# First attention of a two-layer sequence kernel: queries turned once, row maxima put beside them by small transfers

## The reference, cut to what matters

```python
q = _apply_rope((x @ Wq).reshape(b, t, 32, 16).transpose(0, 2, 1, 3), cos, sin)
k = _apply_rope((x @ Wk).reshape(b, t, 8, 16).transpose(0, 2, 1, 3), cos, sin)
scores = jnp.einsum('bhqd,bhkd->bhqk', q, jnp.repeat(k, 4, axis=1)) / math.sqrt(16)
scores = jnp.where(causal[None, None], jnp.finfo(scores.dtype).min, scores)
ctx = jnp.einsum('bhqk,bhkd->bhqd', jax.nn.softmax(scores, axis=-1), jnp.repeat(v, 4, axis=1))
return ctx.transpose(0, 2, 1, 3).reshape(b, t, 512) @ Wo
```

## Time and profile before

| | us |
|---|---|
| median of 3 runs | 1359.84 (1358.13 to 1361.63) |
| span of the profiled execution | 1357.2 |
| PE busy | 1320.4 (97%) |
| VectorE busy | 1036.8 (76%) |
| ScalarE busy | 721.1 (53%) |
| GpSimd busy | 712.1 (52%) |

### The profile page before, as it was taken

How to read it: one execution, slowest core, us unless ns; L and a number is a source line. 1 busy time by engine, 2 the same in 40 slices (tenths; PEclk the granted TensorE clock), 3 DMA queues, 4 the chain that set the end, 5 groups by cost and what they waited for, 6 DMA issues and landing times. The chain is left out here.

```text
span 1357.2 us, 20247 instructions
## 1 busy us (share of the span) xinstructions
PE 1320.4 (97%) x6683; PEld 1055.9 (78%) x6683; DVE 1036.8 (76%) x2438; ACT 721.1 (53%) x1558; POOL 712.1 (52%) x641
## 2 busy tenths in 40 slices
PE   8899999998999999999999999999999999899999
PEld 6666667755776788888888888888888888688877
DVE  8888888876678887787787778777877878775553
ACT  3488887784454544454445545444544455443433
POOL 5589997773646443542444344335424433256643
PEclk9999999999999999999999999999999999999999
DMA  4000000101102110110111101101101001112222
GB/s 147 1 1 1 2 1 2 32 17 55 40 1 78 32 39 9 39 40 17 32 32 31 33 16 32 40 8 35 45 17 32 24 3 46 29 45 59 66 69 84
DMA packets 53335, 45.08 MB, mean 33 GB/s; under 512 B 4400, under 2 KB 42672, under 8 KB 52976
## 3 DMA queue, kind: packets, MB, share of 16 engines
q1 hardware_dynamic: 53232, 43.79, 10.9%
HBM read 41.69 MB, written 2.10 MB: 32 GB/s over the span
## 5 line engine op out<-in xcount | busy, mean ns | idle before, releaser
L1973 POOL TENSOR_TENSOR a_p_lo<-a_prob,a_p_hi 128x512 fp32r<-128x512 f32 x160 | 202.9, 1293 | 21.4 <-ACT a_p_hi L1817 20.7
L244 DVE CUSTOM_DVE_ANT_0 a_score<-a_score,mask_w 128x384 f32<-128x384 f32 (+3 forms) x384 | 196.6, 558 | 9.7 <-PE a_score L1396 7.0
L738 ACT ACTIVATE a_pt_hi<-a_ring 128x512 fp32r<-128x512 f32 x160 | 93.9, 597 | 161.8 <-PE a_ring L422 161.8
L896 POOL TENSOR_TENSOR a_rot_a<-a_rot_a,a_rot_b 128x512 f32<-128x512 f32 x79 | 102.3, 1295 | 146.5 <-DVE a_rot_b L600 146.5
L729 ACT ACTIVATE a_prob<-a_score,a_nmax 128x128 f32<-128x128 f32 (+3 forms) x256 | 132.0, 529 | 57.9 <-DVE a_nmax L244 57.8
L365 PE MATMUL a_xo<-h_hi,w_both 128*128 128x512 f32 x384 | 150.5, 392 | 1.8 <-DVE a_rot_b L600 1.4
L367 PE MATMUL a_xo<-h_hi,w_both 128*128 128x512 f32 x384 | 150.2, 391 | 0.0
L366 PE MATMUL a_xo<-h_lo,w_both 128*128 128x512 f32 x384 | 149.5, 389 | 0.0
L901 POOL TENSOR_TENSOR a_p_lo<-a_rot_a,a_p_hi 128x512 fp32r<-128x512 f32 x79 | 102.3, 1296 | 65.7 <-ACT a_p_hi L755 65.7
L580 DVE TENSOR_TENSOR a_pt_lo<-a_ring,a_pt_hi 128x512 fp32r<-128x512 f32 x160 | 108.6, 687 | 32.1 <-ACT a_pt_hi L738 31.1
L574 DVE TENSOR_SCALAR a_prob<-a_prob,a_rinv 128x128 f32<-128x128 f32 (+3 forms) x256 | 107.8, 464 | 4.8
(11 more groups left out here) (424 smaller groups left out, 3655.0 us busy)
## 6 DMA issues: line engine op xcount, KB each, us to landing
raw<-in_L_attn_wq SPq DMA_DIRECT2D x32, 256.0 KB, 2.9
raw<-in_L_attn_wo SPq DMA_DIRECT2D x32, 256.0 KB, 2.6
raw<-in_L_gate_up_t SPq DMA_DIRECT2D x20, 256.0 KB, 3.1
raw<-in_L_down_t SPq DMA_DIRECT2D x20, 256.0 KB, 3.0
raw<-in_L_attn_wk SPq DMA_DIRECT2D x8, 256.0 KB, 2.9
raw<-in_L_attn_wv SPq DMA_DIRECT2D x8, 256.0 KB, 2.9
out<-x SPq DMA_DIRECT2D x8, 256.0 KB, 2.5
x<-in_L_attn_x SPq DMA_DIRECT2D x3, 512.0 KB, 8.6
```

What stands on the lines that cost most here:

```text
L244: return nc.vector.tensor_tensor_reduce(scores, scores, m.mask_w[:, T - n:T], -1.0, LARGE, ALU.add, ALU.min, to)
L896: nc.gpsimd.tensor_tensor(of_a, of_a, of_b, ALU.add).then_inc(summed, 1)
L1973: nc.gpsimd.tensor_tensor(p_lo[:, mm % NP, :], prob[:, mm % NE, :], p_hi[:, mm % NP, :].bitcast(F32), ALU.subtract).then_inc(p_ready, 1)
```

## The change

- A pair of heads now fills eight slots instead of two times four: queries high, high, low, fourth for the first head and fourth, high, high, low for the second; keys high, low, high, ones and ones, high, low, high. The two fourth slots of a pair are neighbours, so the four values that a head pair needs (high and low part of two maxima) are rows 62 to 65 once turned. `query_high` and `key_high` write the high parts in two operations each where one stood, `query_low` the low parts in two.
- The second turn of the queries, GpSimd's `put_maxima`, and VectorE's 128x512 copy to `q_max` are gone. `q_rows` has four buffers and serves both kinds of scores.
- VectorE's `split_maxima` makes the high and the low part of `nmax` (two operations of 128x8, the second waits for the first). PE's `turn_maxima` turns these 16 columns in one transpose. VectorE's `read_maxima` copies 16x128 to `mx`. SyncE issues four transfers a tile, one for each query head of the group, of 4 rows of 128 values (2 KB), from `mx` to rows 62 to 65 of `q_rows`. The first `turned_scores` of a tile waits for them.
- SyncE's order: the maxima of 32 tiles, with the `L0_b13e` loads ahead of tile 28's and the gate-up loads ahead of tile 31's; the latter now wait for the last turn of queries.
- `c_hi` and `c_lo` have one buffer instead of two. The calls within a unit stand in a new order on PE, VectorE and ScalarE.

```diff
+def query_high(nc, m, t, rotated):
+    for c in range(2):
+        last = nc.scalar.activation(m.q2[t][:, :, c:c + 6:5, :], paired(rotated[:, 0:NG * HPG * HD0]), ACT.Copy,
+                                    scale=float(HD0) ** -0.5)
+    return last
 def query_low(nc, m, t, rotated):
-    return nc.vector.scalar_tensor_tensor(m.q2[t][:, :, 1, :], rotated[:, 0:NG * HPG * HD0].rearrange("p (h n) -> p h n", n=HD0),
-                                          float(HD0) ** -0.5, m.q2[t][:, :, 0, :].bitcast(F32), ALU.mult, ALU.subtract)
+    for x in range(2):
+        last = nc.vector.scalar_tensor_tensor(m.q2[t][:, :, 5 * x + 2, :], paired(rotated[:, 0:NG * HPG * HD0])[:, :, x, :],
+                                              float(HD0) ** -0.5, m.q2[t][:, :, 5 * x, :].bitcast(F32), ALU.mult, ALU.subtract)
+    return last
...
-    NE, NP, NQ = 3, 4, 2
+    NE, NP, NQ = 3, 4, 4
...
+            for n in range(QT * NU):
+                if n == QT * (PAIRS + 3):
+                    sp.wait_ge(c_turned, QT)
+                    for g in range(4):
+                        sp.dma_start(b_raw[32 * g:32 * (g + 1), :], inp["L0_b13e"]).then_inc(m.b_loaded, 16)
+                if n == QT * NU - 1:
+                    sp.wait_ge(q_turned, QT * NU)
+                    for part in range(2):
+                        load_gate_up_part(sp, m, inp, part, m.w_loaded[part])
+                sp.wait_ge(mx_read, n + 1)
+                for h in range(HPG):
+                    sp.dma_start(q_rows[MAX_AT:MAX_AT + 4, n % NQ, h, :].bitcast(F32),
+                                 mx[4 * h:4 * (h + 1), n % 2, :].bitcast(F32)).then_inc(max_put[n % 2], 16)
...
+            def turn_maxima(u, i):
+                n = QT * u + i
+                pe.wait_ge(halved, 2 * (n + 1))
+                claim_qkbank(mx_read, n + 1)
+                nc.tensor.transpose(qkbank[0:2 * X2 * HPG, 0:P],
+                                    halves[:, i % 2, :, :, :].bitcast(F32).rearrange("p h x e -> p (h x e)"),
+                                    m.ident[:, :]).then_inc(qm_turned, 1)
...
                 if x == 0 and j == 0:
-                    pe.wait_ge(qm_read, QT * u + i + 1)
+                    pe.wait_ge(max_put[i % 2], MAX_PUT * ((QT * u + i) // 2 + 1))
...
-                turn_queries(u - 1, 3, 1)
+                turn_maxima(u - 1, 3)
                 weigh(u - 1, 1, 1, 1)
                 turned_scores(u - 1, 2, 0, 2)
-                turned_scores(u - 1, 2, 1, 2)
                 if u:
                     turn_keys(u)
+                weigh(u - 1, 2, 0, 0)
                 turn_back(u - 1, 1)
-                weigh(u - 1, 2, 0, 0)
+                turned_scores(u - 1, 2, 1, 2)
                 weigh(u - 1, 2, 1, 0)
-                weigh(u - 1, 2, 0, 1)
                 if tail:
                     turn_tile(QT)
+                weigh(u - 1, 2, 0, 1)
+                scores(u, 0, 0, 0)
                 turned_scores(u - 1, 3, 0, 0)
...
-            def read_queries(u, i):
+            def split_maxima(u, i):
...
+                both = nmax[:, i % 2, :, :].rearrange("p x h -> p h x")
+                hi, lo = halves[:, i % 2, :, :, 0], halves[:, i % 2, :, :, 1]
+                dve.wait_ge(score_read, scored_by[n])
+                if n >= 2:
+                    dve.wait_ge(qm_turned, n - 1)
+                nc.vector.tensor_copy(hi, both).then_inc(halved, 1)
+                dve.wait_ge(halved, 2 * n + 1)
+                nc.vector.tensor_tensor(lo, both, hi.bitcast(F32), ALU.subtract).then_inc(halved, 1)
+
+            def read_maxima(u, i):
...
+                nc.vector.tensor_copy(mx[0:rows, n % 2, :], qkbank[0:rows, 0:P]).then_inc(mx_read, 1)
```

More of the change, by code:

```diff
@@ L1395, in scores @@
                 if per == 1:
-                    nc.tensor.matmul(out[:, 0:n], q_rows[:, bank, :], k_rows[:, u % 2, x, 0:n], start=True,
+                    nc.tensor.matmul(out[:, 0:n], q_rows[:, (QT * u + i) % NQ, bank, :], k_rows[:, u % 2, x, 0:n], start=True,
                                      stop=True).then_inc(scored, 1)
@@ L1417, in turned_scores @@
                 out = turned[mm % 2][:, :].rearrange("p (h n) -> p h n", h=HPG)
-                last = nc.tensor.matmul(out, k_rows[:, u % 2, x, j * P:(j + 1) * P], q_max[:, (QT * u + i) % NQ, :, :],
+                last = nc.tensor.matmul(out, k_rows[:, u % 2, x, j * P:(j + 1) * P], q_rows[:, (QT * u + i) % NQ, :, :],
                                         start=True, stop=(j < i))
@@ L1511, in _ @@
                     turn_rows(2)
+                scores(u, 1, 0, 1)
+                if tail:
                     turn_tile(QT + 1)
-                scores(u, 1, 0, 1)
+                turn_maxima(u, 0)
                 scores(u, 1, 1, 0)
                 scores(u, 1, 1, 1)
-                turn_queries(u, 2, 0)
+                turned_scores(u - 1, 3, 0, 2)
                 turn_back(u - 1, 2)
-                turned_scores(u - 1, 3, 0, 2)
+                turn_queries(u, 2)
                 turned_scores(u - 1, 3, 1, 2)
@@ L1543, in _ @@
                     project_tile(first)
+                weigh(u - 1, 3, 0, 2)
+                turned_scores(u, 0, 1, 0)
+                scores(u, 3, 0, 0)
+                if first is not None:
                     turn_tile(first + 1)
@@ L1716, in _ @@
                     nc.vector.memset(m.a_st[:, :, :].bitcast(F32), 0.0).then_inc(a_cleared, 1)
+                maxima(u, 1, 1, 0)
+                maxima(u, 1, 1, 1)
+                split_maxima(u, 1)
                 maxima(u, 2, 0, 0)
@@ L1741, in _ @@
                 maxima(u, 2, 1, 3)
+                split_maxima(u, 2)
                 if first is not None:
@@ L1778, in _ @@
                 read_keys(u + 1)
-                take_heads(u, 1)
                 if u == NU - 1:
                     low_row(1)
+                maxima(u + 1, 0, 0, 0)
+                take_heads(u, 1)
+                maxima(u + 1, 0, 1, 0)
+                if u == NU - 1:
                     make_row(2)
-                maxima(u + 1, 0, 0, 0)
-                maxima(u + 1, 0, 1, 0)
+                split_maxima(u + 1, 0)
                 maxima(u + 1, 1, 0, 0)
                 read_heads(u, 2)
-                read_queries(u + 1, 0)
+                read_maxima(u + 1, 0)
         @block.scalar
```

239 lines of the change are left out of this document (109 added, 130 removed).

## The result

The changed kernel takes 1378.39 us (median, 1376.86 to 1379.55) where the kernel before takes 1360.57 in the same comparison: ratio 1.0128, 95% interval 1.0113 to 1.0143, so 17.8 us slower. The profiled execution took 1376.86 us with a span of 1375.1, 17.9 above that of before. The sign of the forecast (1369.0, +9.1) was right, the size was not, and the time lies above the range.

What follows compares the result with a forecast made beforehand. GpSimd, with PE close, was taken to bound units 0 to 3 and PE units 5 and 6; VectorE would become the bound. Terms +8.0, +1.9, -1.3, 0 and +0.5 gave +9.1: 1369.0 us, range 1350 to 1377.

Steps and rivals of the forecast that it cites:

- units 5 and 6: First attention, with batch 0's out-projection: PE 32.1 and VectorE 32.4 us a unit, about 32.8 together, so -1.3 us for both.
- the last stretch: Unit 7's end and the tail: one tile's split, VectorE no bound there, new orders free in themselves: 0 us.
- unit 4: First attention, between units 0 to 3 and the out-projection units: VectorE sets 29.9 us, so +1.9 us.
- The mechanism: In `split_maxima`, VectorE's cast waits for GpSimd's running operation and the dependent subtraction for about a whole further one.
- rival A: First attention: VectorE not held up, split 0.4 us, units of about 26.0 us, 1351.4 us in all; chance 0.22.
- Rival B: In `split_maxima` only one of two waits occurs, split about 1.1 us: no change, 1356.5 us; chance 0.13.
- The price of a split: VectorE's `split_maxima`: waits of 0.55 and 1.0 us plus 0.15 of work, 1.7 us a tile, bounds 0.4 and 2.7.
- The unit: Units 0 to 3 of the first attention: VectorE 28.7 us busy plus 0.6 idle, 29.3 for 27.29, +8.0 for four.
- break-even: Units 0 to 3: the split's cost on VectorE at which a unit keeps its present time, 1.2 us a tile.
- The projection stage: Before the first attention: `query_low` and `query_high` become two operations each, together +0.5 us.
- The transfers: SyncE's four issues a tile: last landing 3.6 us after `mx_read`, just hidden behind PE's matmuls while VectorE sets the pace.
- Rival C: First attention: VectorE free, but late landings hold PE at `turned_scores`: 1370 us at 3.2 us, 1383 at 3.9; chance 0.07.

Runs made afterwards that it cites:

- two mended kernels: Changed kernel with split from PSUM (two transfers) or on GpSimd (one transfer), VectorE's old last-unit order and one-operation `query_low`: 1357.37 and 1357.08 us.
- f_lo's place back: Changed kernel with only `fold_low` put back ahead of `add_tile(QT + 3)` in VectorE's order of the last unit: 1378.47 us, ratio 1.0138.

## Why the prediction was wrong, point by point

The time was put at +9.1 us and the span grew by 17.9. Of the 8.8 us between them, units 0 to 3 make 2.4, units 5 and 6 make 3.8, the last stretch 3.3, and unit 4 takes 0.7 off.

- **The mechanism** held. VectorE's SBUF-to-SBUF operations wait for GpSimd's running one, and the dependent one for a whole further one (1.18 us in the timeline above), as rows 5 and 7 had it. The Trainium skill (GPSIMD Engine Reference, section 8, Key points) names the shared SBUF interfaces, and the traces agree: 1.23 and 1.18 us beside a running GpSimd, 0.17 beside an idle one. The Trainium skill's rule in section 4.1 of that page (Engine selection) sends elementwise work to VectorE, which in this kernel was rival A with 1351 us; here the measurement decides, and the kernel with the split on GpSimd was 17.6 us faster than the one with it on VectorE.
- **Rival B**, with only one of the two waits, isn't the case in units 1 to 4, where the subtraction waits whenever the CAST does. It is what happens in tile 2 of units 5 to 7 (the last two of them at 256.70 and 291.35 us: CAST 0.33 and 1.29, subtraction 0.17 both times).
- **The price of a split** was 1.7 us a tile; it is 1.29 in units 1 to 3 (0.61 + 0.68). The averaging over GpSimd's 85% took every split for a random hit. In fact tiles 0 and 2 pay 2.4 and 2.0, while tiles 1 and 3 pay 0.4 in every unit: the engines run in step, and a tile's split meets nearly the same place of GpSimd's sequence each time.
- **The unit** was forecast at 29.3 us and is 29.08 in units 1 and 2, but the way there failed. VectorE was to be full (28.7 busy and 0.6 idle, over 95%). It is busy for 26.4 and idle for 2.7. The step that failed is that the idle time of the bounding engine stays at 0.6 us. While VectorE stands in a split, PE runs out of score banks or stops at the turn (1.17 us in tile 0), and VectorE waits for PE elsewhere in the unit (1.44 us at one score bank, 119.14 us). That the one wait brings about the other is argued from the orders, not shown by a run. The kernel with the later turn shows that moving the turn alone doesn't win the time back. By the sum's own break-even (1.2 us a tile) a split of 1.29 would have cost 0.4 us a unit, where units 1 and 2 lost about 2. That the unit came out near 29.3 is therefore luck: a split taken 0.4 us a tile too dear made up for idle time taken 2.1 us too short. Units 0 and 3 lost more (3.8 and 2.8): +10.4 for the four in place of +8.0.
- **Units 5 and 6** were to gain 1.3 us and lost 2.5. This is the largest miss, 3.8 us. The sum had PE at 32.1 and VectorE at 32.4 us a unit, two engines near the bound. In the trace VectorE is busy for only 28.5, with splits of some 1.0 us a tile. What failed are PE's two terms: its busy time fell by 0.1 us a unit and not by 1.3, and it is idle for 1.4 us a unit where it had none. Of these 2.7 us 2.3 are at `turn_maxima` of tile 0, behind the split (PE's only listed wait in 224.93 to 291.31 us):

```profile
PE a_qkbank L1408 <- DVE a_halves L1674: 2.3, 2, 1.2
```

Even with the split away from VectorE these units are 63.5 and 63.7 us in the two mended kernels, against 63.92: PE's busy time fell by 0.5 and 0.6 us a unit there. Unit 4 was +1.2 for a forecast of +1.9.
- **The last stretch** was put at 0 and cost 3.3 us. The step that failed is the sentence that the new orders "cost nothing by themselves": it was argued from a full VectorE queue in the units, and the order of the last unit wasn't read. Putting it back gives 3.3 us in the medians, the same size (2.9 by the ratios).
- **The projection stage** was put at +0.5. The halving of `query_low` costs 2.0 us in the changed kernel and 4.8 in the kernel before. The rows of the split's rival (rows 5, `query_low` at 1.07 us) were at hand and applied to the small operations only. In the profile the first `a_p_lo` is just 0.5 us late, as forecast, and in the kernel with one `query_low` it comes at 71.09 us, 1.6 earlier than before. Whether the rest of the change brings such a gain is open: these are single profiles with the lower clock at different places (0.83 at 10 to 20 us before, 0.83 at 30 to 40 in that kernel), and the two mended kernels, with one `query_low` too, start at 72.87 and 71.67 us.
- **The transfers** came out right, in part by luck: 3.6 us were forecast from copy to last landing, 3.5 are seen at PE (and 4.0 at 170.19), but from 0.58 us an issue and not 0.42, with a shorter landing. They are not quite hidden: PE and its weight loader together wait 8.1 us in 15 times for them, PE alone 2.0 in 4. Rival C is no cause here, though in the kernels with the split from PSUM two issues less a tile were worth 3.1 us. Its 1383 us for a landing of 3.9 us stands without its working; its own steps give 1379 to 1388.
- **Rival A** asked for VectorE to be free, and then a unit of 26.0 us and 1351.4. With that condition met, the mended kernels give units of 26.8 and 27.3 us and 3.4 us less than before, where rival A had 8.4 less. Only the first of them also relieves GpSimd, as rival A had it. The price was 5 us too good: PE's busy time in units 0 to 3 fell by 0.84 and 0.67 us a unit (108.37 to 105.03 and 105.70) and not by 1.3.

The parts add up. By the ratios, the idea without the three costs is worth -3.4 us (mended kernels), the split on VectorE costs 16.6 (against the split on GpSimd), the last stretch 2.9 and `query_low` 2.2: +18.3 us, with 17.4 by the ratio of the changed kernel. They were measured in different kernels, and needn't add exactly. What stays open is the clock at the stage change: it mostly falls behind the longer idle time, but with an exception on either side, and its share in the 3.3 us was seen in single profiles only.

## What to carry to other kernels

Count the VectorE operations that read and write SBUF while GpSimd streams, not their elements: each can cost a whole GpSimd operation, and dividing one in two pays it twice; read from PSUM where the data pass there anyway, or leave the work on GpSimd. In a loop of engines with few buffers between them, busy time plus today's idle time isn't the new period: here the idle time of the delayed engine was 2.7 us and not 0.6. A change that rewrites orders is to be costed in its last unit too, where a long operation put ahead of a short one delays the stage behind it.

## What the runs showed of the hardware

- VectorE operations of 128x8 with both ends in SBUF, 0.17 us when GpSimd is idle, take up to 1.30 us when it isn't; three in a row took 1.06, 1.20 and 1.28 us. Copies and subtractions from PSUM in the same stretch keep their times (16x128 in 0.27, 8x128 in 0.28 us), and so does GpSimd's `a_p_lo` (1.288 us in mean, 1.291 before).
- The waiting goes both ways when VectorE's operation is long: in the kernel before, a GpSimd operation of 128x512 that began at 38.15 us took 1.74 us in place of 1.29, while VectorE finished one of 128x512 with both ends in SBUF.
- Issues of transfers from SBUF to SBUF took SyncE 0.57 to 0.58 us for 2 KB, 0.60 to 0.62 for 4 KB and 0.63 for 8 KB, where the 1 KB load of rows 8 took 0.42.
- Behind 2.9 us of idle time TensorE's matmuls of 128x512 came every 0.43 us instead of every 0.23, which is the lower of its two levels (1.2 and 2.4 GHz); the mean granted clock of the 5 us stretches was 0.77 and 0.89. With the same 2.9 us of idle time in the kernel with f_lo's place back, the first matmuls came every 0.23 us. Behind 2.85 to 2.95 us of idle time the clock fell within 4 us in eight of nine kernels, behind 1.93 us in one of five.
